# A pre-norm scan and mixture-of-experts kernel: a new order of rounding, remainders, routing steps and mixing, and two more PSUM banks for a quad's down part

## The chip, the cores and the metric

The kernel runs on one core of one Trainium2 chip. The metric is the device time of one execution in microseconds (us), the median over runs; lower is better. TensorE is the matrix engine, VectorE, ScalarE and GpSimd are the other compute engines, and SyncE (SP) issues most of the transfers.

## What is computed

The input is 4 x 1024 tokens of 256 features. Two blocks follow one another, each on a layer-normed copy of its input and added to it. The reference, cut to what matters:

```python
def attn(x, w_qkva, gamma):
    h = rmsnorm(x, gamma)                     # 256 features
    q, kv, a = split(h @ w_qkva.T)            # 256 each
    a = sigmoid(a)
    y = associative_scan(lambda l, r: (r.a * l.a, r.a * l.kv + r.kv), (a, kv), axis=1)
    return q * y
def ffn(x, router_w, w_gate, w_up, w_down, sw_gate, sw_up, sw_down):
    logits = x @ router_w.T                   # 7 experts
    top_vals, top_idx = top_k(logits, 2)
    w = softmax(top_vals)
    y_e = (silu(x @ w_gate[e]) * (x @ w_up[e])) @ w_down[e]    # hidden size 1024
    return sum of w * y_e over a token's two experts + the same with sw_* (shared expert)
x = x + attn(layernorm(x), ...)
x = x + ffn(layernorm(x), ...)
```

All of it is in float32.

## The kernel before

**Precision.** A matrix product in float32 is made of three products of rounded operands (float32r): hi x hi, hi x lo and lo x hi, where hi is the rounded value and lo the remainder. Rounding is ScalarE's work (`round_w`, `x_hi`, `h_hi`), remainders are VectorE's and GpSimd's. `w_both` holds an expert's rounded weights and their remainders for gate, up and down (parts 0, 1, 2); there are two such buffers. `w_raw` lies in the place of the remainders: the raw weights land there and are turned into the remainders in place. The loads of the next expert but one can start when a buffer's gate and up parts have been used.

**Stages.** Behind the scan block come in this order: two shared slots and four shared quads (the shared expert on 256 and 512 tokens at a time), two lone blocks (128 tokens of one expert each, plain float32), one more shared quad ("LATE"), four lone blocks, twelve routed quads, eight routed single slots, and two shared quads as the tail. A slot is 256 sorted tokens of one expert, a quad 512.

**A quad** has eight steps over the hidden size (128 each), then the down part. In step j TensorE makes gate and up with 12 matmuls of 512 columns (L1127) into banks 0 to 3, ScalarE the silu (L844), VectorE the product h32 (`gate`, L1700), ScalarE the rounded `h_hi` (L849), VectorE the remainder `h_lo` (`rest`, L1706). TensorE may be two steps ahead of the product. In the early quads h32 lies in SBUF, in the others in bank 7. In two of the steps VectorE transposes the next tokens' rows (`turn_x`, L1330) into bank 6, ScalarE rounds them (`x_hi`), VectorE makes their remainder (`x_lo`, L1344). The down part has two halves of two tiles. The first (`down_wide`) uses banks 4 and 5: one matmul of 512 columns takes h_hi against rounded weights and remainders side by side (L1105), one of 256 adds h_lo x hi (L1108). The second half works in bank 6 alone, with three matmuls of 256 columns (L1146).

**The order written out by hand.** Each engine's program is a list with waits on semaphores. ScalarE rounds the next expert's weights in a routed quad behind `h_hi` of steps 0 to 5: up, up, gate, gate, down, down. VectorE makes the remainder of up in two halves (`split_half`, L1661) behind steps 3 and 4, in a single slot behind the fourth pair. GpSimd does, per quad: `gather_ahead` of one unit (indirect DMA, L642), the remainder of gate (`split_lo`, L618), the second gather, the remainder of down, then two scatters of finished rows (L655). `scatter_y` also gives ScalarE leave to fill `y_rows` again (`y_free`). SP puts gathered rows to DRAM, loads them back in the layout for the transposition, and then issues the next weights: up, gate (L412), and down (L418).

**y of a routed quad.** ScalarE copies the remainder columns of banks 4 and 5 (L861), VectorE adds the others (L1773); of bank 6 ScalarE copies all (L865).

**Routing.** VectorE chooses the experts, ranks the tokens and moves their places (`rank_kinds` to `shift`), then makes lists of rows by one-hot matmuls: eight chunks of eight tiles (`hot_rows`, `hot_cols`), which TensorE multiplies in `list_part` (L1058), in bank 7. `take_lists` writes the row numbers of the gathers (L1625), `take_targets` those of the scatters, `owners` the experts of the slots. All are spread between the steps of the quads 2, 4 and 6.

**Tail.** In the two last quads SP fetches each token's two expert rows (`load_got`, L538 and L541), in four rounds of 6, 12, 12 and 2 tiles. ScalarE multiplies them by their weights (`weigh`, L904), VectorE adds the two and then adds the sum to `resid` (`mix`, L1646 and L1648), and SP stores.

```python
for j in range(JH):                                       # ScalarE, a quad
    act.activation(silu...); act.wait_ge(gated, q + 3)
    act.activation(h_hi...)
    if nxt is not None and j < 6:
        round_w((1, 1, 0, 0, 2, 2)[j], nxt[0], nxt[1], j % 2)
```

## Time and profile before

| | us |
|---|---|
| median of 3 runs | 1114.69 (1114.10 to 1115.27) |
| the profiled execution | 1114.16 |
| its span on the core | 1112.4 |
| TensorE busy | 1019.9 (92% of the span) |
| VectorE busy | 637.9 (57%) |
| ScalarE busy | 477.9 (43%) |
| GpSimd busy | 407.6 (37%) |

A busy share is an average over stages. The granted clock says at which share of 2.4 GHz TensorE ran; at its lower level, 1.2 GHz, the value of a moment is 0.5. "Idle before" is the time that an engine stood still before an instruction, with the instruction that released it. Instructions of one engine overlap by about 0.1 us in the records.

### The profile page before, as it was taken

Reading aid. Unit: us, or ns where it says so; the run is one execution under the profiler, and the core shown is the slowest. Engines: PE = TensorE matmul, PEld = TensorE weight load, DVE = VectorE, ACT = ScalarE, POOL = GpSimd, SP = SyncE. Lnnn points to the kernel's source line nnn. Section 1 sums busy time; section 2 is a strip of 40 time slices with the busy share of each in tenths; the row PEclk is TensorE's granted clock in tenths of the full one; section 3 lists DMA queues with packets and bytes.
Section 4 is the critical chain, followed back from the end, with each engine's and each line's share of the span. In section 5 each row is a group of like instructions: output and inputs, shape, how many; then the busy total and the mean of one; then the engine's idle time right before and its main releaser. Section 6 shows DMA issues by size and latency. Waiting matters only on the chain.

```text
span 1112.4 us, 16252 instructions
## 1 busy us (share of the span) xinstructions
PE 1019.9 (92%) x5757; PEld 882.9 (79%) x5757; DVE 637.9 (57%) x1037; ACT 477.9 (43%) x778; POOL 407.6 (37%) x258
## 2 busy tenths in 40 slices
PE   7999999998999999999999999999999688888897
PEld 6788978877989978777877887787779677777776
DVE  7997677876333353464346444644553655656566
ACT  4554342231233244354435443543454444455474
POOL 3234000002101443554455345634653666445300
PEclk9999999999999999999999999999999988888899
DMA  8324110002865744424443444344434555343544
GB/s 293 95 77 113 41 28 10 20 1 82 255 246 179 269 158 166 152 85 160 165 142 94 165 160 141 95 165 165 133 96 168 175 214 198 132 155 118 180 143 142
DMA packets 145907, 155.08 MB, mean 139 GB/s; under 512 B 75321, under 2 KB 134210, under 8 KB 138690
## 3 DMA queue, kind: packets, MB, share of 16 engines
q1 hardware_dynamic: 139120, 136.08, 37.5%
q0 software_dynamic: 6720, 18.36, 5.1%
q8 instruction: 28, 0.46, 0.2%
q14 instruction: 21, 0.17, 0.0%
q10 hardware_dynamic: 18, 0.01, 0.0%
HBM read 127.67 MB, written 26.74 MB: 139 GB/s over the span
## 4 chain that ended last, share of the span: by engine, by line
PE 49%; DVE 23%; ACT 15%; issue 10%; DVEq 0%; DMA 0%; POOL 0%; SPq 0%; ACTq 0%
PE ps L1127 16%; PE ps L1146 9%; DVE ps L1700 7%; DVE w_both L1661 6%; PE ps L1105 5%; PE ps L1083 5%; PE ps L1166 4%; ACT w_both L788 4%; ACT h_hi L849 3%; PE ps L990 3%; ACT silu L844 3%; PE ps L1108 3%; PE ps L1174 2%; ACT silu L816 2%; DVE y_sb L1312 2%
## 5 line engine op out<-in xcount | busy, mean ns | idle before, releaser
L1127 PE MATMUL ps<-xs_hi,w_both 128*128 128x512 f32 x1216 | 402.8, 405 | 41.4 <-DVE ps L1700 33.5
L1127 PEld LDWEIGHTS ps<-xs_hi,w_both 128*128 128x128 f32 x1216 | 236.2, 194 | 108.1 <-DVE ps L1700 49.6
L618 POOL TENSOR_TENSOR w_both<-w_raw,w_both 128x2048 fp32r<-128x2048 f32 x45 | 227.3, 5058 | 95.0 <-ACT w_both L788 86.3
L1127 PE MATMUL ps<-xs_lo,w_both 128*128 128x512 f32 x608 | 243.4, 400 | 0.0
L1700 DVE TENSOR_TENSOR ps<-ps,silu 128x512 f32<-128x512 f32 x160 | 111.3, 696 | 191.8 <-ACT silu L844 135.4
L642 POOL DMA_INDIRECT x_stage<-z_rows,idx_x x70 | 82.1, 1173 | 296.4 <-DVE idx_x L1625 143.8
L1706 DVE TENSOR_TENSOR h_lo<-ps,h_hi 128x512 fp32r<-128x512 f32 x160 | 110.7, 692 | 106.9 <-ACT h_hi L849 85.5
L1105 PE MATMUL ps<-w_both,h_hi 128*128 128x512 f32 x464 | 165.5, 399 | 1.8 <-DVE h_lo L1706 1.8
L1083 PE MATMUL ps<-xs_hi,w_both 128*128 128x256 f32 x640 | 130.1, 303 | 32.8 <-DVE w_both L1661 32.0
L849 ACT ACTIVATE h_hi<-ps 128x512 fp32r<-128x512 f32 x128 | 76.6, 598 | 146.4 <-DVE ps L1700 146.4
L1083 PEld LDWEIGHTS ps<-xs_hi,w_both 128*128 128x128 f32 x640 | 110.6, 210 | 35.5 <-issue 35.4
L1127 PEld LDWEIGHTS ps<-xs_lo,w_both 128*128 128x128 f32 x608 | 118.5, 195 | 22.8
L844 ACT ACTIVATE silu<-ps 128x512 f32<-128x512 f32 x152 | 90.1, 593 | 103.4 <-PE ps L1127 103.4
L655 POOL DMA_INDIRECT expert_rows<-y_rows,idx_y x70 | 69.8, 997 | 175.4 <-DVE y_rows L1773 69.8
L788 ACT ACTIVATE w_both<-w_raw 128x1024 fp32r<-128x1024 f32 x126 | 130.8, 1051 | 0.0
L1108 PE MATMUL ps<-w_both,h_lo 128*128 128x256 f32 x464 | 130.4, 281 | 0.0
L1146 PE MATMUL ps<-w_both,h_hi 128*128 128x256 f32 x608 | 111.6, 286 | 0.0
L1661 DVE TENSOR_TENSOR w_both<-w_raw,w_both 128x1024 fp32r<-128x1024 f32 x42 | 106.8, 2558 | 0.0
L1105 PEld LDWEIGHTS ps<-w_both,h_hi 128*128 128x128 f32 x464 | 87.3, 188 | 23.5 <-DVE h_lo L1706 3.0
L1146 PEld LDWEIGHTS ps<-w_both,h_hi 128*128 128x128 f32 x608 | 95.8, 194 | 0.8
L1083 PE MATMUL ps<-xs_lo,w_both 128*128 128x256 f32 x320 | 96.2, 301 | 0.0
L1108 PEld LDWEIGHTS ps<-w_both,h_lo 128*128 128x128 f32 x464 | 87.8, 189 | 0.8
(222 smaller groups left out, 1166.2 us busy)
## 6 DMA issues: line engine op xcount, KB each, us to landing
w_raw<-in_L_ffn_w_up_dram SPq DMA_DIRECT2D x20, 1024.0 KB, 4.9
w_raw<-in_L_ffn_w_gate_dram SPq DMA_DIRECT2D x20, 1024.0 KB, 7.1
w_raw<-in_L_ffn_w_down_dram SPq DMA_DIRECT2D x20, 1024.0 KB, 5.5
sorted_rows<-x_stage SPq DMA_DIRECT2D x32, 256.0 KB, 2.2
x_rows<-sorted_rows SPq DMA_DIRECT2D x128, 64.0 KB, 1.9
w_spare<-in_L_ffn_w_up_dram SPq DMA_DIRECT2D x6, 1024.0 KB, 5.2
w_spare<-in_L_ffn_w_gate_dram SPq DMA_DIRECT2D x6, 1024.0 KB, 8.7
w_spare<-in_L_ffn_w_down_dram SPq DMA_DIRECT2D x6, 1024.0 KB, 9.6
```

The costliest lines, as they stand in the source:

```text
L618: pool.tensor_tensor(w_lo[buf][:, k, :], w_raw[buf][:, k, :], w_hi[buf][:, k, :].bitcast(F32), ALU.subtract).then_inc(wlo_ready[k], 1)
L788: ins = act.activation(w_hi[buf][:, k, cols], w_raw[buf][:, k, cols], ACT.Copy)
L844: act.activation(silu[:, par, :, :], ps[:, 2 * par, :].rearrange("p (j n) -> p j n", j=2), ACT.Silu).then_inc(silu_ready, 1)
L849: act.activation(h_hi[:, j, :].rearrange("p (j n) -> p j n", j=2), h32_of(par, early), ACT.Copy).then_inc(hhi_ready, 1)
L1083: last = pe.matmul(o, w[:, part, at[kd]:at[kd] + P], unit(xx, h)[:, kd, :], start=i == 0, stop=i == len(terms) - 1)
L1105: pe.matmul(ps[:, 4 + t, :].rearrange("p (b d) -> p b d", d=D), h_hi[:, j, t * P:(t + 1) * P], both[:, :, 2, j * D:(j + 1) * D], start=j = ...
L1108: last = pe.matmul(ps[:, 4 + t, 0:D], h_lo[:, j, t * P:(t + 1) * P], hi[:, 2, j * D:(j + 1) * D], start=False, stop=j == JH - 1)
L1127: last = pe.matmul(ps[:, 2 * (j % 2) + part, :], w[:, part, kd * H + j * P:kd * H + (j + 1) * P], xx[:, h // 2, kd, :], start=i == 0, stop ...
L1146: last = pe.matmul(ps[:, 6, (t - ST) * D:(t - ST + 1) * D], a[:, j, t * P:(t + 1) * P], w[:, 2, j * D:(j + 1) * D], start=j == 0 and i == ...
L1661: ins = dve.tensor_tensor(w_lo[buf][:, 1, cols], w_raw[buf][:, 1, cols], w_hi[buf][:, 1, cols].bitcast(F32), ALU.subtract)
L1700: dve.tensor_tensor(h32_of(par, early), up, silu[:, par, :, :], ALU.mult).then_inc(gated, 1)
L1706: dve.tensor_tensor(out, h32_of(par, early), hi.bitcast(F32), ALU.subtract).then_inc(h_ready, 1)
```

## The change

The numbers that follow are all in the diff.

- Rounding: in quads ScalarE rounds gate behind silu of steps 0 and 1, up behind silu of steps 3 and 4, and down behind the last step; in slots gate, gate, up, up behind the four silus. SP loads gate before up.
- Remainders: VectorE makes both halves of up behind the last step of a quad. GpSimd makes the remainder of gate ahead of the first gather.
- Down part: in all quads but the early ones the second half has the form of the first, in banks 6 and 7. ScalarE copies, and VectorE adds, as for the first half. The fourth shared quad becomes an early one.
- Routing: the lists use float16 and one value for a token in place of two, in groups of 16 tiles; the steps move to other places, and the last three groups (`take_lists`, `take_targets`, `owners`) too. SP issues `load_lone(1)` behind two loads of x.
- Mixing: VectorE does own tiles and round 0 with two scalar_tensor_tensor a tile; in rounds 1 and 2 ScalarE weighs the other tiles and GpSimd adds them.

```diff
@@ SP
-                for k in (1, 0):
+                for k in (0, 1):
                     sp.dma_start(parts_of(w_raw[b])[k], sources[k]).then_inc(raw_in[b][k], 16)
...
-            for i in range(2):
-                load_lone(i)
+            load_lone(0)
             for u in range(2):
                 load_x(LATE + u, SA - 2 + u, z_dram, u)
+            load_lone(1)
...
+            sp.wait_ge(mixed, TOP * (ST + OTHERS[0]))
+            store_others(0)
+            load_got(2)
+            store_own(0)
+            sp.wait_ge(mixed, TOP * (ST + OTHERS[0] + ST))
+            load_got(3)
+            store_own(1)
...
@@ GpSimd
+                split_lo(0, r + 2, 1 - r % 2)
                 gather_ahead(i + 4)
-                split_lo(0, r + 2, 1 - r % 2)
                 gather_ahead(i + 5)
                 split_lo(2, r + 2, 1 - r % 2)
                 scatter_y(i)
                 scatter_y(i + 1)
...
+            for j in (1, 2):
+                for b in range(2):
+                    many = OTHERS[j] // 2
...
+                    pool.wait_ge(weighed, TOP * done)
+                    pool.tensor_tensor(sums, sums, got[:, j % 2, ps_, 1, :], ALU.add).then_inc(others_summed, many)
+                    pool.wait_ge(others_summed, done)
+                    pool.tensor_tensor(rows, rows, sums, ALU.add).then_inc(others_mixed, many)
@@ ScalarE, slot
+                    if nxt is not None:
+                        round_w((0, 0, 1, 1)[p], nxt[0], nxt[1], p % 2)
                     act.wait_ge(gated, q + 3)
...
-                    if nxt is not None:
-                        round_w((1, 1, 0, 0)[p], nxt[0], nxt[1], p % 2)
@@ ScalarE, quad
+                    if nxt is not None and j in (0, 1, 3, 4):
+                        round_w(j // 3, nxt[0], nxt[1], j % 3)
                     act.wait_ge(gated, q + 3)
...
-                    if nxt is not None and j < 6:
-                        round_w((1, 1, 0, 0, 2, 2)[j], nxt[0], nxt[1], j % 2)
...
+                if nxt is not None:
+                    for half in range(2):
+                        round_w(2, nxt[0], nxt[1], half)
...
                     act.wait_ge(y_free, r + 1)
-                    act.wait_ge(down_free, n + 2)
-                    act.activation(y_rows[:, 1, :, :], ps[:, 6, :].rearrange("p (t d) -> p t d", d=D), ACT.Copy
-                                   ).then_inc(down_free, 1)
+                    act.activation(y_rows[:, 1, :, :], ps[:, 6:8, D:2 * D], ACT.Copy).then_inc(y_half, 1)
...
-            quad(NB0, NB0 % 4, between={4: lambda: weigh(0, range(0, 2)), 5: lambda: weigh(0, range(2, 4)),
-                                        6: lambda: weigh(0, range(4, 6))})
-            for p in range(0, 12, 4):
-                weigh(1, range(p, p + 4))
+            quad(NB0, NB0 % 4, between={6: lambda: weigh(1, (ST,)), 7: lambda: weigh(1, (ST + 1,))})
+            weigh(1, range(ST + 2, ST + OTHERS[1]))
             quad(NB0 + 2, (NB0 + 2) % 4, turns=(), between={
-                j: lambda j=j: weigh(2, range(2 * j - 2, 2 * j)) for j in range(1, 7)})
-            weigh(3, range(2))
+                j: lambda j=j: weigh(2, (ST + j,)) for j in range(JH)})
+            weigh(2, range(ST + JH, ST + OTHERS[2]))
@@ TensorE, quad, second half of the down part
                 for t in range(ST, 2 * ST):
                     for j in range(JH):
+                        if not early:
+                            last = down_wide(j, both, hi, (t,))
+                            continue
...
-                at = {2: {}, 4: {1: [0], 6: [1], JH: [2]}, 6: {1: [3], 2: [4], 6: [5], JH: [6, 7]}, 8: {}}[n]
+                at = {2: {}, 4: {1: [0], JH: [1]}, 6: {0: [2], 1: [3], 6: [4], JH: [5]}, 8: {0: [6], 2: [7]}}[n]
@@ VectorE, mixing
+                dve.wait_ge(got_in[u], (64, 64, 128, 96)[j])
+                first_of = mixes[0]
+                for k in range(TOP):
+                    for i, p in enumerate(ps_):
+                        if k:
+                            dve.wait_ge(mixed, first_of + i + 1)
...
+                        dve.scalar_tensor_tensor(out=row, in0=got[:, u, p, k:k + 1, :],
+                                                 scalar=mix_w[:, k, t:t + 1], in1=row,
+                                                 op0=ALU.mult, op1=ALU.add).then_inc(mixed, 1)
@@ VectorE, quad
-                    if nxt is not None and j in (3, 4):
-                        split_half(*nxt, j - 3)
+                    if nxt is not None and j == JH - 1:
+                        split_up(*nxt)
...
-                    dve.wait_ge(y_half, routed)
-                    dve.tensor_tensor(y_rows[:, 0, :, :], ps[:, 4:6, 0:D], y_rows[:, 0, :, :], ALU.add
-                                      ).then_inc(down_free, 1)
+                    for half in range(2):
+                        dve.wait_ge(y_half, routed + half)
+                        dve.tensor_tensor(y_rows[:, half, :, :], ps[:, 4 + 2 * half:6 + 2 * half, 0:D],
+                                          y_rows[:, half, :, :], ALU.add).then_inc(down_free, 1)
+                    dve.wait_ge(down_free, n + 3)
@@ VectorE, where the routing steps and the mixing stand
             betweens = {
-                2: {0: lone_targets, 2: find_pairs, 3: find_over, 4: move_pairs, 5: move_alone,
-                    6: move_over, 7: move_on, "down": rows_of_first, "half": first_lists},
-                4: {0: lambda: hot_rows(1), 3: lambda: hot_cols(1), 6: lambda: hot_rows(2), 7: lambda: hot_cols(2),
-                    "down": lambda: lists(3), "half": lambda: lists(4)},
-                6: {1: lambda: hot_rows(5), 3: lambda: hot_cols(5), 6: lambda: hot_rows(6), 7: lambda: hot_cols(6),
-                    "down": lambda: lists(7), "half": last_lists}}
+                2: {0: pair_targets, 3: lone_places, 6: lone_targets, 7: find_pairs, "down": move_all,
+                    "half": first_lists},
+                4: {0: lambda: hot_rows(1), 3: lambda: hot_cols(1), 7: lambda: pick(1),
+                    "down": lambda: (halves_of(1), lists(2)), "half": lambda: lists(3)},
+                6: {0: lambda: hot_rows(4), 3: lambda: hot_cols(4), 6: lambda: hot_rows(5), 7: lambda: hot_cols(5),
+                    "down": lambda: (lists(6), owners()), "half": lambda: lists(7)}}
...
-            quad(n, n % 4, turns=ahead_of(n), kind="lone", shared=n, skip=0)
+            quad(n, n % 4, shared=n, early=True, skip=0, between={
+                3: take_lists, 6: take_targets, "down": lambda: turn(n, n % 4, 2, loads(n + 2), 0, "lone"),
+                "half": lambda: turn(n, n % 4, 3, loads(n + 3), 0, "lone")})
...
             quad(NB0, NB0 % 4, turns=ahead_of(NB0), shared=SA, between={
-                5: lambda: mix(0, range(0, 2)), 7: lambda: mix(0, range(2, 6)),
-                "half": lambda: mix(1, range(0, 2))})
+                6: lambda: mix(0, (0,)), 7: lambda: mix(0, (1,)), "down": lambda: mix(0, range(2, 6)),
+                "half": lambda: mix(1, (0, 1))})
...
+                4: lambda: mix(2, (0,)), 5: lambda: mix(2, (1,)), 6: lambda: mix(3, (0,)), 7: lambda: mix(3, (1,))})
```

## Rows read from the trace of the kernel before

**Rows 1.** Busy time by stage: early quads 2 to 6, fourth, routed, slots, tail.

```profile
core 0: us, PE busy (x) PEld busy (x) DVE busy (x) ACT busy (x) POOL busy (x), PEclk, DMA share, GB/s
148.50:262.98 114.48, 108.12 (x594) 90.46 (x593) 90.41 (x184) 32.25 (x55) 2.31 (x2) 0.99 0.05 12
262.98:296.17 33.19, 33.19 (x179) 28.70 (x178) 14.74 (x29) 9.58 (x16) 4.04 (x4) 1.00 0.79 239
392.79:844.85 452.06, 420.94 (x2115) 351.76 (x2114) 218.88 (x300) 200.47 (x312) 223.83 (x119) 0.97 0.43 142
844.85:1032.67 187.82, 151.24 (x1026) 143.18 (x1025) 112.14 (x112) 90.30 (x129) 106.73 (x41) 0.89 0.46 158
1032.67:1112.40 79.73, 70.42 (x352) 58.57 (x352) 48.40 (x67) 44.59 (x98) 6.14 (x3) 0.97 0.50 162
```

**Rows 2.** Who TensorE waited for: us in total, times, longest.

```profile
PE ps L1127 <- DVE ps L1700: 33.5, 16, 2.5
PE ps L1083 <- DVE w_both L1661: 32.0, 7, 4.6
```

**Rows 3.** The chain that ended last, in two routed quads: start, us, what.

```profile
603.91 4.44 PE ps L1127 x12
...
613.99 5.76 PE ps L1146 x48
619.75 2.76 PE ps L1127 x12
```

**Rows 4.** VectorE in a routed quad, timeline: start, us, instruction.

```profile
600.27 2.98 DVE L1661 TENSOR_TENSOR w_both<-w_raw,w_both 128x1024 fp32r<-128x1024 f32 x1
603.17 0.69 DVE L1700 TENSOR_TENSOR ps<-ps,silu 128x512 f32<-128x512 f32 x1
```

**Rows 5.** VectorE, GpSimd and SP in single slots, timeline.

```profile
883.17 6.69 DVE L1661 TENSOR_TENSOR w_both<-w_raw,w_both 128x1024 fp32r<-128x1024 f32 x2
...
883.56 10.71 POOL L618 TENSOR_TENSOR w_both<-w_raw,w_both 128x2048 fp32r<-128x2048 f32 x2 [2.71 <-ACT w_both L788]
...
903.28 1.03 POOL L642 DMA_INDIRECT x_stage<-z_rows,idx_x  x1 [0.30 <-issue]
...
910.86 0.37 SPq L412 DMA_DIRECT2D w_raw<-in_L_ffn_w_up_dram  x1
```

**Rows 6.** ScalarE in a routed quad, timeline.

```profile
624.59 1.06 ACT L788 ACTIVATE w_both<-w_raw 128x1024 fp32r<-128x1024 f32 x1
625.53 0.59 ACT L844 ACTIVATE silu<-ps 128x512 f32<-128x512 f32 x1
626.98 0.60 ACT L849 ACTIVATE h_hi<-ps 128x512 fp32r<-128x512 f32 x1 [0.85 <-DVE ps L1700]
```

**Rows 7.** GpSimd's second remainder in a routed quad, timeline.

```profile
605.52 4.62 POOL L618 TENSOR_TENSOR w_both<-w_raw,w_both 128x2048 fp32r<-128x2048 f32 x1
```

**Rows 8.** DMA issues of the page: count, KB each, median us from issue to landing.

```profile
w_raw<-in_L_ffn_w_up_dram SPq DMA_DIRECT2D x20, 1024.0 KB, 4.9
w_raw<-in_L_ffn_w_gate_dram SPq DMA_DIRECT2D x20, 1024.0 KB, 7.1
...
w_spare<-in_L_ffn_w_gate_dram SPq DMA_DIRECT2D x6, 1024.0 KB, 8.7
```

**Rows 9.** Timeline: the lists done; the first lone weights issued.

```profile
257.90 0.20 DVE L1625 CAST idx_x<-rows_f 128x70 int32<-128x70 f32 x1
...
274.16 0.36 SPq L447 DMA_DIRECT2D w_spare<-in_L_ffn_w_up_dram  x1
```

**Rows 10.** Two stretches of the tail, columns as in rows 1.

```profile
1054.00:1056.00 2.00, 2.00 (x11) 1.65 (x10) 1.81 (x3) 2.00 (x6) 0.00 (x0) 1.00 0.96 303
...
1076.00:1078.00 2.00, 2.00 (x10) 1.65 (x10) 1.33 (x3) 1.49 (x4) 0.00 (x0) 1.00 0.72 247
```

**Rows 11.** Timeline: a scalar_tensor_tensor of the routing; the fetch of round 2.

```profile
179.06 0.48 DVE L1534 SCALAR_TENSOR_TENSOR tmp<-keep,over_to,tmp 128x256 f32<-128x256 f32 x1
...
1064.66 0.36 SPq L538 DMA_DIRECT2D got<-expert_rows  x1
```

More of the change, by code:

```diff
@@ L1100, in slot, with down_wide @@
                 last.then_inc(down_psum, 1)
-            def down_wide(j, both, hi):
-                for t in range(ST):
+            def down_wide(j, both, hi, tiles=range(ST)):
+                for t in tiles:
                     pe.matmul(ps[:, 4 + t, :].rearrange("p (b d) -> p b d", d=D),
```

149 lines of the change are left out of this document (74 added, 75 removed).

## The prediction

> **What bounds the kernel now.** I read the stages first, then who makes TensorE wait, then one routed quad engine by engine. The table by stage [rows 1] shows TensorE busy nearly all the time in every stage, so the way to look is what its best pace is and which stages miss it. The shared quad from 262.98 has no gap at all: 33.19 us, clock 1.00. That is the floor of a quad of four tiles. The twelve routed quads take 452.06 us, 37.67 each, so 4.5 above the floor. The eight single slots take 187.82, or 23.48 each. The waits [rows 2] name the losers: 33.5 us in 16 waits for the gating product on VectorE (L1700), 32.0 in 7 of up to 4.6 for the remainder of the up weights (L1661).
>
> Inside a routed quad the chain [rows 3] gives the pace: twelve matmuls of 512 columns take 2.76 us, but 4.44 after the long wait (the engine was idle before it and runs at the lower level, 1.2 GHz, for a while), and the 48 matmuls of the second down half 5.76. So a quad loses 2.5 us of waiting and 1.7 of low clock. VectorE [rows 4] shows the cause: after step 4 it starts the second half of the up remainder at 600.27, and it takes 2.98 instead of 1.2, since GpSimd is in its own remainder; the next gating product starts only at 603.17. The same in the slots [rows 5]: two halves take 6.69 on VectorE while GpSimd does 10.71 for two remainders. One engine's operation stands still for the whole of the other's, in turn. TensorE, done with the slot before, waits 4.6 for them [rows 2].
>
> **The change part by part.** Times below count from TensorE's start of the quad or slot; pace 2.72 a step in a quad, 2.88 a pair in a slot (11.5 for the whole gate and up part, then 5.65 of down).
>
> *Routed quads.* ScalarE's silu and h_hi take 0.6 each, a rounding half 1.05, and between silu and h_hi it now waits 0.85 for the product [rows 6]. Put in that wait, a rounding half costs 0.2 more than nothing; silu, rounding and h_hi are 2.3 us of a 2.72 step, and the two steps with an x_hi have no rounding. VectorE has two operations of 0.7 a step, and in four of eight steps one more of about that length (transposition or x_lo): at most 2.2 of 2.72 without the remainder. The up remainder goes to the end: h_lo of step 7 ends at 24.8, both halves at 27.2, while TensorE is in the down part until 33.1. So the wait of 2.5 and the low clock of 1.7 are gone. What is late next: GpSimd's second remainder waits for the two rounding halves at the end (26.0), yields to VectorE until 27.1, and takes 4.6 [rows 7], to 31.7; only then does it reach the scatter that lets ScalarE copy the second half of y (needed at 33.2). That holds with 1.5 us. With y in banks 6 and 7 VectorE must also add the second half (34.0 to 34.7) before it may write bank 7 in the next quad, whose first gating product isn't due before 36.7: hidden. The 32 matmuls in place of 48 stream the same columns; the first half does that in 33.19-8x2.72-5.76=5.67, so 0.1 is gained. Gather and transfer: the fifth step's transposition ends at 17.5, gathers at 20.0, and 6.55 us later (gather end 904.31 to the issue at 910.86 [rows 5]) the gate weights are issued, at 26.6; the first of two loads lands in 4.9 [rows 8], at 31.5, and is wanted at 36.8. Hidden by 5 us. New quad: 33.1. 12 x (37.67-33.1) = **-54.9**.
>
> *Slots.* VectorE's remainder starts at 14.75, before GpSimd asks (16.05), and ends at 17.15, just when TensorE finishes (17.17). Without more a slot takes 17.2. But the gather now stands behind the gate remainder, and this closes a ring: gate weights land, two roundings with h_hi and silu between (3.15), remainder 4.6, two gathers 2.5, put, load and issue 6.55, landing 4.9: 21.8 us from one load to the next. ScalarE stands at the first rounding from 3.7 until the landing at 8.9, so everything behind it is late: rounding 1.05, h_hi 0.6, silu of the second pair 0.6 and its product 0.7, so TensorE's fourth pair starts at 12.0 instead of 8.6; with 2.9 for the pair, 1.4 of low clock after a wait of 3.4 and 5.65 of down part the slot ends at 21.9. Slots 1 to 4 hang on gathers and take 21.9; slot 0 has its weights from the quads, and slots 5 to 7 load rows that need no gather: 17.2. 4x17.2+4x21.9=156.4. **-31.4**.
>
> *Shared quads and routing.* The three quads with the lists take 114.48 [rows 1]. Each chunk loses one of VectorE's two products, and most steps move behind the gate part. I count 34.1 (the steps that stay, twelve or so of 0.2 and two of 0.45, leave 0.9 of lateness over 33.2), 37.9 (the first list chunk is made 2.3 us after TensorE wants it, plus 1.5 of low clock, plus two list parts of 0.5, estimated from eight times 140 columns at the pace of 2.76 for twelve times 512) and 35.1 (four list parts; the owners' steps, which held VectorE between the down halves, fit before the next quad's first product): 107.1, **-7.4**. The fourth quad pays 1.2 for two list parts and for taking the lists at step 3. There the lists come late: done at 17.3 of that quad. Before, SP issued the first lone expert's weights 16.3 us after the lists (257.90 to 274.16 [rows 9]): now at 33.4, when TensorE is nearly done (34.4). Landing takes 7.1 to 9.1 (gate is second: 7.1 with w_raw, 8.7 for w_spare [rows 8]), so TensorE waits 7.6 and pays 1.4 of clock. **+10.2**. The second lone expert's weights follow behind eight loads of x, by 304 of the trace's time, before they are wanted at 309.
>
> *Tail.* N is its start; today it takes 79.73. The fetches of y's rows keep the DMAs busy until 1056, N+23.4 [rows 10]. ScalarE now asks for round 1 in step 6 (N+21.3) and waits 2.4; five of its tiles are weighed at N+30. VectorE mixes by scalar_tensor_tensor, 0.5 each (0.48 in the routing [rows 11]): 12 for round 0, eight of them done by N+30. Then GpSimd starts its adds, 4.62x1280/2048=2.9 each. If these two block one another like the remainders [rows 5], each of VectorE's last four operations lets one add by: done at N+43; then 1.4+2+1.4 more, so the last quad's first product ends at N+48.7, where TensorE wants it at N+39.1. The fetch of round 2 starts at N+43.3, lands some 12.7 later as now (1064.66 to about 1077.4 [rows 10, 11]), at N+56, and ScalarE stands before it, so step 3 starts at N+58.3. Five steps, the down part, 1.4 of clock and 1.7 of one more block end TensorE at N+86.3, the last adds and the store take 5: N+91.3, **+11.5**. No row shows scalar_tensor_tensor against GpSimd: without a block the same count gives N+78, -1.7. I take the first, since the nearest row is the remainder, also two operands from SBUF.
> The Trainium skill ("SBUF — State Buffer", Who interferes with whom) says that any VectorE instruction with two SBUF inputs contends with a GpSimd instruction that reads SBUF, whole instruction for whole instruction. The trace agrees for tensor_tensor [rows 5]; by the rule the tail is +11.5, and GpSimd's help with mixing is a loss.
>
> Sum: -54.9-31.4-7.4+10.2+11.5 = -72.0. The profiled execution is 1114.16 (span 1112.4 and 1.8 around it), 0.5 under the median of the runs: 1114.2-72 = **1042**.
>
> **The rivals.**
> 1. Tail without the block (a scalar operand form might take turns more finely). For: no row shows it. Against: the remainders. 1042-13=1029.
> 2. The ring in the slots doesn't bind, because load or gather is shorter than its rows: 1042-4x4.7=1023. Against: every term has a row, and 4.9 is already the first load's median [rows 8].
> 3. The quads keep a part of their wait: product and remainder of h meet the transposition in steps 1 and 4 (VectorE is 0.4 to 0.6 late there, against 1.3 of slack). One wait of 1.3 a quad: +16, 1058; if it also draws the low clock (1.7), 1078.
> 4. The slower side: bank 7. Its chain in a quad is GpSimd reaching the scatter (31.7), y copy 0.6, y add 0.7, gating product 0.7, with some 0.3 between; TensorE wants that product at 38.5, so it costs from 36.2 on, one for one. To give back 72 us it has to be 6.0 a quad, so GpSimd at 42.2, 10.5 later than counted: 1114 and more. That is two further whole remainders; against it speaks that GpSimd is busy 223.83 us in twelve quads [rows 1], 18.7 of 33 each.
> 5. The change doesn't do it: the wait in the quad comes from something other than VectorE's order, as a late load. Against: the product starts the moment the remainder ends (603.17) [rows 4]. 1114-31-5=1080 or so.
>
> **How the numbers follow.** The sum as worked out 50% (1042); rival 1 15%, rival 2 8%, rival 3 20%, rivals 4 and 5 with other mishaps 7%. Bounds of the unknown terms: tail -13 to +3, lone load -2 to +3, first list chunk -4, landing in the ring up to 7.1 instead of 4.9 (+9). From 1018 to 1066 lie rivals 1 and 2, the first half of 3, and these bounds; the second half of 3 and rivals 4 and 5 are left out. A measurement here tells about 0.2%, 2 us, from no change; only rival 4, or several mishaps at once, reaches it: faster 0.96, same 0.01, slower 0.03.
>
> **What would show it.** Right: quads of 33.1 to 33.5 with clock 1.00 and no wait for L1700; up remainders of 1.2 each behind step 7; slots of 17.2, four of 22 whose ScalarE idles before a rounding; TensorE waiting once, 7 us, for the first lone weights; VectorE's mixing operations of 3 us beside GpSimd's adds in the tail. Wrong: a quad over 34.5, ScalarE idle before the second y copy (rival 4), or slots all at 17.

## The result, and the profile after

The changed kernel takes 1051.95 us (median of four runs, 1051.18 to 1052.50) against 1114.39 for the kernel before beside it: ratio 0.9441, 95% interval 0.9425 to 0.9457. The profiled execution took 1051.96, with a span of 1050.2. That is 62.2 us of span less; 72 were forecast. One of the four executions of experiment 9 below took 1967.32 us and is left out of its numbers; what held it up isn't known.

Busy time by stage of the changed kernel, columns as in [rows 1]: quads 2 to 6, the fourth shared quad, routed quads, slots, tail.

```profile
148.84:252.93 104.09, 102.33 (x586) 87.57 (x585) 79.78 (x161) 32.89 (x55) 0.00 (x0) 1.00 0.05 11
252.93:288.78 35.85, 34.28 (x190) 28.83 (x186) 21.96 (x46) 9.62 (x16) 5.34 (x5) 1.00 0.16 41
396.07:793.60 397.53, 397.53 (x1923) 334.00 (x1921) 206.96 (x311) 205.07 (x312) 216.47 (x119) 1.00 0.49 161
793.60:956.79 163.19, 146.27 (x1027) 139.08 (x1026) 78.12 (x112) 90.00 (x128) 101.91 (x41) 0.93 0.55 187
956.79:1050.20 93.41, 72.34 (x322) 58.78 (x320) 53.22 (x71) 36.27 (x75) 29.86 (x11) 0.90 0.42 138
```

Against [rows 1], in us of span, every stage from one profiled execution of each kernel:

| stage | before | after | measured | forecast |
|---|---|---|---|---|
| up to quad 2 | 148.50 | 148.84 | +0.3 | 0 |
| quads 2, 4, 6 (lists) | 114.48 | 104.09 | -10.4 | -7.4 |
| fourth shared quad | 33.19 | 35.85 | +2.7 | +1.2 |
| two lone blocks | 21.01 | 31.80 | +10.8 | +9.0 |
| LATE and four lone blocks | 75.61 | 75.49 | -0.1 | 0 |
| twelve routed quads | 452.06 | 397.53 | -54.5 | -54.9 |
| eight slots | 187.82 | 163.19 | -24.6 | -31.4 |
| tail | 79.73 | 93.41 | +13.7 | +11.5 |
| sum | 1112.4 | 1050.2 | -62.2 | -72.0 |

The routed quads are the easy reading: busy 397.53 of 397.53, clock 1.00, 33.13 each. Who TensorE waits for after the change (total, times, longest):

```profile
PE ps L1101 <- DVE ps L1733: 16.8, 4, 7.8
PE ps L1145 <- DVE ps L1733: 11.8, 3, 6.7
PE ps L1187 <- issue: 9.1, 1, 9.1
```

The 16 waits for the product in [rows 2] were 12 in the routed quads (30.2 us) and 4 in the tail (3.4). The 12 are gone, and so are the 7 for the up remainder and an eighth at the tail's start (4.6). In their place stand four waits in the slots (L1101), three in the tail (L1145) and one before the first lone block (L1187). The line named in the first two, VectorE's product, is only the last link; the causes follow.

**Slots.** The slots, counted from 0 as in the prediction, take 17.47, 27.96, 21.37, 23.55, 21.32, 17.20, 17.16 and 17.16. Slot 1 begins at 811.07. ScalarE there (timeline: start, us, instruction, idle before):

```profile
814.24 0.60 ACT L837 ACTIVATE silu<-ps 128x512 f32<-128x512 f32 x1 [2.61 <-PE ps L1101]
824.76 1.06 ACT L809 ACTIVATE w_both<-w_raw 128x1024 fp32r<-128x1024 f32 x1 [9.92 <-DMA w_raw<-in_L_ffn_w_gate_dram]
```

GpSimd and SP ahead of it:

```profile
801.67 0.97 POOL L664 DMA_INDIRECT expert_rows<-y_rows,idx_y  x1 [7.12 <-DMA expert_rows<-y_rows,idx_y]
802.95 0.98 POOL L664 DMA_INDIRECT expert_rows<-y_rows,idx_y  x1 [0.30 <-issue]
803.95 4.65 POOL L627 TENSOR_TENSOR w_both<-w_raw,w_both 128x2048 fp32r<-128x2048 f32 x1
808.76 1.88 POOL L651 DMA_INDIRECT x_stage<-z_rows,idx_x  x1 [0.16 <-issue]
810.94 1.03 POOL L651 DMA_INDIRECT x_stage<-z_rows,idx_x  x1 [0.30 <-issue]
...
814.61 0.40 SPq L457 DMA_DIRECT2D sorted_rows<-x_stage  x1
...
819.45 0.37 SPq L414 DMA_DIRECT2D w_raw<-in_L_ffn_w_gate_dram  x1
```

This is the ring of the prediction: remainder, gathers, rows to DRAM and back, and only then the next weights, which land at 824.7 while ScalarE and all behind it stand still.

**Tail.** VectorE and GpSimd, timeline:

```profile
984.43 12.28 DVE L1679 SCALAR_TENSOR_TENSOR resid<-got,mix_w,resid 128x256 f32<-128x256 f32 x10
...
998.27 2.66 DVE L1679 SCALAR_TENSOR_TENSOR resid<-got,mix_w,resid 128x256 f32<-128x256 f32 x4
...
987.13 3.10 POOL L714 TENSOR_TENSOR got<-got 128x1280 f32<-128x1280 f32 x1 [23.84 <-ACT got L924]
990.38 2.96 POOL L716 TENSOR_TENSOR resid<-resid,got 128x1280 f32<-128x1280 f32 x1
993.30 3.13 POOL L714 TENSOR_TENSOR got<-got 128x1280 f32<-128x1280 f32 x1
996.58 2.88 POOL L716 TENSOR_TENSOR resid<-resid,got 128x1280 f32<-128x1280 f32 x1
```

Ten mixing operations take 12.28. The first seven are over at 987.41, 2.98 after the start and just when GpSimd begins; the other three last 3.20, 3.17 and 3.17, each ending 0.3 after one of GpSimd's adds. With nothing on GpSimd beside them (experiment 8) the same ten take 4.16:

```profile
987.53 4.16 DVE L1667 SCALAR_TENSOR_TENSOR resid<-got,mix_w,resid 128x256 f32<-128x256 f32 x10
```

### The profile page after: what moved, and what is told of

Same layout as the page of the kernel before. It is cut to its first block, busy times and chain, and to the rows that moved or that the text cites. A ratio compares the mean times of both kernels' runs of the same rounds, so it can differ in the third digit from the quotient of the medians.

```text
span 1050.2 us, 15774 instructions
## 1 busy us (share of the span) xinstructions
PE 990.5 (94%) x5517; PEld 859.6 (82%) x5517; DVE 594.0 (57%) x1048; ACT 474.5 (45%) x754; POOL 419.2 (40%) x267
## 4 chain that ended last, share of the span: by engine, by line
PE 67%; DVE 11%; issue 8%; POOL 5%; DMA 4%; ACT 2%; SPq 1%; DVEq 0%; POOLq 0%; ACTq 0%
PE ps L1145 32%; PE ps L1123 11%; PE ps L1126 6%; PE ps L1101 5%; PE ps L1187 4%; PE ps L1007 3%; POOL w_both L627 3%; PE ps L1195 2%; DMA got<-expert_rows 2%; DVE y_sb L1333 2%; PE ps L991 1%; DVE resid L1679 1%; PE ps L1167 1%; DVE h_early L1733 1%; DVE h_lo L1739 1%
## 5 line engine op out<-in xcount | busy, mean ns | idle before, releaser
L1145 PE MATMUL ps<-xs_hi,w_both 128*128 128x512 f32 x1216 | 384.7, 394 | 12.5 <-DVE ps L1733 11.8
L1145 PEld LDWEIGHTS ps<-xs_hi,w_both 128*128 128x128 f32 x1216 | 230.6, 190 | 63.2 <-DVE ps L1733 13.1
L1123 PE MATMUL ps<-w_both,h_hi 128*128 128x512 f32 x704 | 250.2, 399 | 1.0 <-DVE h_lo L1739 0.9
L1145 PE MATMUL ps<-xs_lo,w_both 128*128 128x512 f32 x608 | 238.6, 392 | 0.0
L1126 PE MATMUL ps<-w_both,h_lo 128*128 128x256 f32 x704 | 197.5, 281 | 0.0
L651 POOL DMA_INDIRECT x_stage<-z_rows,idx_x x70 | 73.1, 1044 | 240.4 <-DVE idx_x L1651 156.4
L1123 PEld LDWEIGHTS ps<-w_both,h_hi 128*128 128x128 f32 x704 | 132.5, 188 | 33.6 <-DVE h_lo L1739 1.8
L1101 PE MATMUL ps<-xs_hi,w_both 128*128 128x256 f32 x640 | 126.3, 296 | 17.7 <-DVE ps L1733 16.8
L809 ACT ACTIVATE w_both<-w_raw 128x1024 fp32r<-128x1024 f32 x126 | 130.5, 1053 | 25.1 <-DMA w_raw<-in_L_ffn_w_gate_dram 25.0
L1145 PEld LDWEIGHTS ps<-xs_lo,w_both 128*128 128x128 f32 x608 | 115.5, 190 | 23.4
L1126 PEld LDWEIGHTS ps<-w_both,h_lo 128*128 128x128 f32 x704 | 133.0, 189 | 0.7
L1101 PEld LDWEIGHTS ps<-xs_hi,w_both 128*128 128x128 f32 x640 | 106.6, 202 | 19.8 <-DVE ps L1733 17.6
L1101 PE MATMUL ps<-xs_lo,w_both 128*128 128x256 f32 x320 | 93.9, 293 | 0.0
L1101 PEld LDWEIGHTS ps<-xs_lo,w_both 128*128 128x128 f32 x320 | 64.7, 202 | 0.0
L1809 DVE TENSOR_TENSOR y_rows<-ps,y_rows 128x512 f32<-128x512 f32 x24 | 16.6, 692 | 75.2 <-ACT y_rows L888 59.5
L1187 PE MATMUL ps<-xs_lone,w_spare 128*128 128x128 f32 x384 | 45.5, 281 | 9.1 <-issue 9.1
```

What stands on the lines that cost most here:

```text
L651: pool.indirect_dma_start(x_stage[:, i % 2, t, :], None, z_dram, bass.IndirectOffsetOnAxis(ap=idx_x[:, c:c + 1], axis=0), bounds_check=N - ...
L809: ins = act.activation(w_hi[buf][:, k, cols], w_raw[buf][:, k, cols], ACT.Copy)
L1101: last = pe.matmul(o, w[:, part, at[kd]:at[kd] + P], unit(xx, h)[:, kd, :], start=i == 0, stop=i == len(terms) - 1)
L1123: pe.matmul(ps[:, 4 + t, :].rearrange("p (b d) -> p b d", d=D), h_hi[:, j, t * P:(t + 1) * P], both[:, :, 2, j * D:(j + 1) * D], start=j = ...
L1126: last = pe.matmul(ps[:, 4 + t, 0:D], h_lo[:, j, t * P:(t + 1) * P], hi[:, 2, j * D:(j + 1) * D], start=False, stop=j == JH - 1)
L1145: last = pe.matmul(ps[:, 2 * (j % 2) + part, :], w[:, part, kd * H + j * P:kd * H + (j + 1) * P], xx[:, h // 2, kd, :], start=i == 0, stop ...
```

## The experiments

The changed kernel is the base of every run but where said; line numbers shift by a few between them. The kernel before had medians of 1115.15 beside experiments 1 to 4, 1114.31 beside 6, 7, 8 and 10, 1114.50 beside 9, 11 and 12, and 1113.51 beside 5.

**1. The quads with the old order.**

```diff
# ScalarE, quad
-  round gate behind silu of steps 0, 1; up behind silu of 3, 4; down at the end
+  round behind h_hi of steps 0 to 5: up, up, gate, gate, down, down
# VectorE, quad
-  if nxt is not None and j == JH - 1: split_up(*nxt)
+  if nxt is not None and j in (3, 4): split_half(*nxt, j - 3)
```

> The changed kernel, with ScalarE's rounding and VectorE's up remainder of the routed quads in the old places (rounding behind h_hi of steps 0 to 5 as up, up, gate, gate, down, down; up remainder behind steps 3 and 4). Theory: this order is where the 54 us of the quads came from. A quad goes from 33.1 back to 37 to 38 us, twelve of them 47 to 56 us: 1099 to 1108 us in all. Rival (banks 6 and 7 or GpSimd's order gave a part): under 1090 us.

Measured: 1118.15, ratio 1.0023 (1.0007 to 1.0039). The routed quads take 461.87, 38.49 each, even 0.8 more than before. With this part of the change undone all the gain is given back, and more than the 1099 to 1108 that were expected. VectorE and GpSimd in one quad of this run:

```profile
606.05 1.22 DVE L1691 TENSOR_TENSOR w_both<-w_raw,w_both 128x1024 fp32r<-128x1024 f32 x1
...
609.83 2.97 DVE L1691 TENSOR_TENSOR w_both<-w_raw,w_both 128x1024 fp32r<-128x1024 f32 x1
612.73 0.69 DVE L1730 TENSOR_TENSOR ps<-ps,silu 128x512 f32<-128x512 f32 x1
...
606.44 5.28 POOL L627 TENSOR_TENSOR w_both<-w_raw,w_both 128x2048 fp32r<-128x2048 f32 x1 [11.62 <-ACT w_both L809]
```

The block of [rows 4] is back within a hundredth: 2.97 for the second half, since GpSimd is in the remainder of gate until 611.72. But a block of 2.5 and 1.7 of low clock make 37.3, not 38.5. Something else is in here too; experiment 5 shows what.

**2. Only VectorE's remainder back between the steps.**

```diff
-  if nxt is not None and j == JH - 1: split_up(*nxt)
+  if nxt is not None and j in (4, 5): split_half(*nxt, j - 4)
```

> The changed kernel, with only VectorE's up remainder of the quads moved, behind steps 4 and 5. Two readings of the old wait: (a) VectorE had no room for 2.4 us between its steps, then a wait returns wherever it stands in the gate part; (b) only the block by GpSimd's remainder (2.98 us in place of 1.2) made it too long. In the new order GpSimd is in its gathers at steps 4 and 5, so by (b) each half takes 1.2 us, VectorE is 0.9 late at step 5 against 1.3 of slack, and the quad stays at 33.1 to 33.4 us: 1050 to 1056 us in all. By (a) a quad is 35 us or more: over 1074 us.

Measured: 1054.07, ratio 0.9453 (0.9435 to 0.9472); the quads 399.16, 33.26 each. With gate rounded first GpSimd's remainder of gate is over before VectorE starts:

```profile
581.02 1.20 DVE L1694 TENSOR_TENSOR w_both<-w_raw,w_both 128x1024 fp32r<-128x1024 f32 x1
...
584.70 1.22 DVE L1694 TENSOR_TENSOR w_both<-w_raw,w_both 128x1024 fp32r<-128x1024 f32 x1
...
573.03 4.64 POOL L627 TENSOR_TENSOR w_both<-w_raw,w_both 128x2048 fp32r<-128x2048 f32 x1
```

So it was never a matter of room on VectorE. With gate rounded first, the place behind the last step, to which the prediction gave the whole gain of a quad, is worth 0.13 a quad.

**3. The rounding behind h_hi again, in the new order.**

```diff
-  if nxt is not None and j in (0, 1, 3, 4): round_w(...)
   act.wait_ge(gated, q + 3)
   act.activation(h_hi...)
+  if nxt is not None and j in (0, 1, 3, 4): round_w(...)
```

> The changed kernel, with only ScalarE's rounding of the quads moved back behind h_hi (still gate in steps 0 and 1, up in 3 and 4, down at the end). Theory: silu, a wait of 0.85, h_hi and rounding are 3.1 us of a 2.72 us step; two such steps in a row make silu 0.4, then 0.8 late, still inside TensorE's slack of 1.3 a step, so the quad stays at 33.1 to 33.5: 1050 to 1056 us in all. Rival: the place inside ScalarE's wait carries much of the quads' gain, 35 us a quad or more: over 1074 us.

Measured: 1053.15, ratio 0.9445 (0.9426 to 0.9464), quads 397.53: the same to the hundredth. Filling ScalarE's idle time with the rounding, as the changed kernel does, is of no use here, since ScalarE isn't what ends last.

**4. The second down half in bank 6 alone, as before.**

```diff
-  if not early: last = down_wide(j, both, hi, (t,)); continue     # TensorE
-  copy of ps[:, 6:8, D:2*D], VectorE adds ps[:, 6:8, 0:D]
+  ScalarE copies ps[:, 6, :] whole
```

> The changed kernel, with the second half of every down part back in bank 6 (48 matmuls of 256 columns, ScalarE copies it whole, VectorE adds nothing). Theory: only the shorter stream counts, 0.1 us a quad, 14 quads: 1.4 us slower in all, 1052 to 1055, and the tail's last adds 0.7 shorter. Rival: the wide form costs by its second add or by bank 7 as a gate for the next quad: then this version is faster, under 1050 us.

Measured: 1052.83, ratio 0.9433 (0.9407 to 0.9459); the quads 398.44, 33.20 each: 0.07 more in each, so 0.9 for all twelve. That is the 0.1 of the prediction, and less than the runs can tell apart.

**5. The old rounding order, VectorE's remainder at the end.** The fourth corner of the first two runs.

```diff
# ScalarE as in experiment 1; VectorE as in the changed kernel
```

> The changed kernel with the quads' rounding as before (behind h_hi of steps 0 to 5: up, up, gate, gate, down, down), but VectorE's up remainder left behind the last step. With the run that moved only the remainder (quads 33.2) and the one that undid both (38.5), this is the fourth corner. Theory: the two edits are alternatives in the quads, since either keeps VectorE's remainder out of the time of GpSimd's remainder of gate while a gating product is due. With up rounded first GpSimd's gate remainder runs from about 14 to 19 of the quad and the one of down from about 23 to 27, so VectorE's two halves at 24.8 are blocked by 2 or 3 us, but under the down part, where nothing waits for them before the next quad's first product at about 36: quads 33.1 to 33.4, time 1050 to 1055, ratio 0.942 to 0.947. Rival: the rounding order costs the quads something by itself (the gather and the loads come later, or ScalarE's six steps with a rounding are too full): quads over 34 and a time over 1063.

Measured: 1103.40, ratio 0.9902 (0.9882 to 0.9923); the quads 448.17, 37.35 each. The expectation fell and its rival held. No product waits for a remainder here, and yet each quad loses 4.2. The block itself is still there: at the end of the quad VectorE's first half takes 4.4 to 4.7, beside GpSimd's remainder of down, but under the down part of TensorE, where nothing waits for it. VectorE, ScalarE, GpSimd and SP in the quad from 582.88:

```profile
613.61 5.54 DVE L1691 TENSOR_TENSOR w_both<-w_raw,w_both 128x1024 fp32r<-128x1024 f32 x2
...
591.45 1.06 ACT L809 ACTIVATE w_both<-w_raw 128x1024 fp32r<-128x1024 f32 x1 [3.53 <-DMA w_raw<-in_L_ffn_w_up_dram]
...
602.48 4.62 POOL L627 TENSOR_TENSOR w_both<-w_raw,w_both 128x2048 fp32r<-128x2048 f32 x1 [8.55 <-ACT w_both L809]
...
620.92 0.36 SPq L414 DMA_DIRECT2D w_raw<-in_L_ffn_w_gate_dram  x1
621.38 0.38 SPq L414 DMA_DIRECT2D w_raw<-in_L_ffn_w_up_dram  x1
...
629.52 1.06 ACT L809 ACTIVATE w_both<-w_raw 128x1024 fp32r<-128x1024 f32 x1 [2.58 <-DMA w_raw<-in_L_ffn_w_up_dram]
```

It is the ring of the slots, closed in the quads. ScalarE rounds up first, but SP now loads up second. Up lands at 591.4; up and gate are rounded by 602.4; then the remainder of gate to 607.1, the gathers behind it to 612.3, and rows out and in until 620; up is issued at 621.4 and lands 8.1 later, at 629.5. That is 38.1 from landing to landing in this quad (37.35 a quad on average), longer than the 33.1 of TensorE's work. ScalarE stands for it in each quad (38.5 us in 12 waits), the product is late, TensorE waits 1.8 to 3.4 (L1142) in eleven of the twelve quads and pays in clock. In experiment 1 this wait is there as well (18.2 us in 12), on top of the block, which fits the 0.8 over the kernel before.

Two things make the ring longer than with gate first. GpSimd can start its remainder of gate 10.9 after the landing, when four halves are rounded, where in the changed kernel the two halves of gate are done 3.8 after the first begins (598.39 to 602.17). And what is rounded first is loaded second and lands 8.1 after its issue, where the first of a pair takes 5.0. With SP's order put back too the ring would be some 35.0 by these numbers, an estimate that no run tried. The edit also moves the rounding of down from the end back between the steps; that wasn't tried by itself either.

The four corners, all with the gathers behind the remainder of gate, us per routed quad:

| | remainder at the end | remainder between the steps |
|---|---|---|
| gate rounded first | 33.13 | 33.26 (experiment 2) |
| up rounded first | 37.35 (experiment 5) | 38.49 (experiment 1) |

**6. The first gather ahead of the remainder of gate, as before.**

```diff
# GpSimd, quad
+  gather_ahead(i + 4)
   split_lo(0, r + 2, 1 - r % 2)
-  gather_ahead(i + 4)
# GpSimd, slot
-  split_lo(0, r + 2, 1 - r % 2)
   if i + 4 < NS + ROUTED: gather_ahead(i + 4)
+  split_lo(0, r + 2, 1 - r % 2)
```

> The changed kernel, with GpSimd's first gather ahead of its gate remainder again, in quads and slots. Theory: in quads nothing changes (33.1 us). In slots the ring opens, but the gate remainder now runs when VectorE wants its up remainder, and the two block one another: VectorE's two halves take 6 us or more, TensorE waits 4 to 5 us a slot, 21 to 24 us each where there are gathers, 17 to 22 in the other four. In all 1050 to 1075 us. Rival: the order of these two makes no difference, 1050 to 1054 us with slots as now.

Measured: 1063.88, ratio 0.9545 (0.9527 to 0.9562). The quads don't care (33.13), the slots take 174.42 in place of 163.19. VectorE and GpSimd in a slot of this run:

```profile
837.54 9.54 DVE L1694 TENSOR_TENSOR w_both<-w_raw,w_both 128x1024 fp32r<-128x1024 f32 x2
...
835.76 9.09 POOL L627 TENSOR_TENSOR w_both<-w_raw,w_both 128x2048 fp32r<-128x2048 f32 x2
```

With the gathers first GpSimd comes late to its remainders and is in them when VectorE wants its own: two halves take 9.54 in place of 2.35, worse than [rows 5]. TensorE waits 5.7 to 6.9 for the remainder in the four slots with gathers, and these take 24.5 to 26.8, more than the 21 to 24 expected.

**7. The ring in the slots opened.** SP issues gate and up ahead of the rows.

```diff
   v = n + 4 - R0
+  if r + 2 <= TURNS: load_gate_up(r + 2, u, n + 1, ...)
   if v < ROUTED: put_and_load(v, u, v // 2)
   else: load_x(n + 4, SA + v - ROUTED, z_dram, u)
-  if r + 2 <= TURNS: load_gate_up(r + 2, u, n + 1, ...)
```

> The changed kernel, with SP issuing the gate and up loads of a single slot ahead of that slot's put and load of gathered rows (they wait for TensorE's gate part alone). Theory of the ring: gate weights land, remainder, gather, put, load, next gate weights closes a ring of about 22 us, which slots 1 to 4 hang on. Cut there, all eight slots take 17.2 to 18.5 us: the slots' 163 us become 138 to 146, 1027 to 1035 us in all. Rival (the transfers themselves, or GpSimd with 16 us of work a slot, set the pace): the slots stay over 20 us, over 1042 us in all.

Measured: 1026.83, ratio 0.9219 (0.9203 to 0.9234), 25.1 us less than the changed kernel. The slots of this run, columns as in [rows 1]:

```profile
795.59:933.27 137.68, 137.61 (x1027) 131.37 (x1026) 78.50 (x112) 90.06 (x128) 101.90 (x41) 1.00 0.67 221
```

17.2 each, no wait, clock 1.00. The weights never needed the rows; they only stood behind them in SP's program.

**8. No adds on GpSimd in the tail.** This run leaves out the adds of the other tiles of rounds 1 and 2, four adds of 5 tiles, so 20 in all (not 22, as the expectation says); its output is missing them.

```diff
-  pool.tensor_tensor(sums, ...); pool.tensor_tensor(rows, ...)      # L714, L716
```

> The changed kernel without GpSimd's adds of rounds 1 and 2 in the tail (22 tiles do not get their experts' part; SP stores them once ScalarE has weighed them). Theory of the block: VectorE's scalar_tensor_tensor stands still for each add of 3 us. Without them ten of them take 5 us instead of 12.3, the last quad's first wait of 6.7 us goes, the fetch of round 2 starts 7 us earlier, and the tail shrinks by 8 to 14 us: 1038 to 1044 us in all. Rival: the fetches set the tail's pace, and it shrinks by less than 4 us, over 1048 us.

Measured: 1039.97, ratio 0.9327 (0.9304 to 0.9350). The tail takes 78.49, where the prediction's count without a block gave 78. Of the 14.9 gained TensorE's end brings 10.6 (74.4 after the tail's start in place of 85.0), and what follows it 4.3 (4.1 in place of 8.4). So the run takes away the block and GpSimd's late end together; it doesn't price them apart.

**9. The mixing as before, all else new.**

```diff
-  scalar_tensor_tensor on VectorE, adds of rounds 1 and 2 on GpSimd
+  ScalarE weighs, VectorE adds with two tensor_tensor (L1646, L1648 of before); SP's stores as before
```

> The changed kernel with the tail's mixing as it was before the change (ScalarE weighs, VectorE adds with tensor_tensor, nothing on GpSimd, SP's order of stores as before); all else stays. If the tail's +13.7 (79.7 to 93.4) comes from the new division of the mixing, the tail takes 78 to 80 from the start of its first quad and the time is 1037 to 1040, ratio 0.931 to 0.934, with no VectorE operation over 1.5 us there. Rival: a part of it comes from what stands ahead of the tail (the shape of the second down half, the last scatters, y of the last slots coming late): then the tail stays over 83 and the time over 1042.

Measured: 1038.36, ratio 0.9311 (0.9282 to 0.9340). Its tail, and VectorE in it:

```profile
959.61:1037.00 77.39, 67.95 (x322) 55.14 (x320) 50.10 (x69) 45.17 (x99) 6.04 (x3) 0.99 0.51 167
```

```profile
1002.36 1.22 DVE L1658 TENSOR_TENSOR got<-got 128x1024 f32<-128x1024 f32 x1
1003.68 1.23 DVE L1660 TENSOR_TENSOR resid<-resid,got 128x1024 f32<-128x1024 f32 x1
```

Two operations of 1.22 serve four tiles, 0.61 a tile; the new form costs VectorE 0.8 to 1.0 a tile even undisturbed (4.16 for five tiles in experiment 8, 1.00 for one at 978.69 in the changed kernel), and 2.5 in the 12.28 for five. So the new mixing costs 16.0 of tail (93.41 against 77.39), and 13.6 of the median time; the stages ahead of the tail were 2.8 longer in this run's profile.

**10 and 11. The first lone weights ahead of the rows; then both.**

```diff
   sp.wait_ge(listed, 1)
+  sp.wait_ge(routed, 1)
+  load_lone(0)
   put_x, load_sorted of units 0 and 1; put_x of 2 and 3
-  sp.wait_ge(routed, 1)
-  load_lone(0)
   load_x of LATE; load_lone(1)             # e12: load_lone(1) right behind load_sorted(1)
```

> The changed kernel, with SP issuing the first lone expert's weights as soon as the lists are done (270.8), ahead of the puts and loads of gathered rows. Theory: they land some 9 us later, long before TensorE wants them at 288.8, so its wait of 9.1 us and about 1 us of low clock go: 1040 to 1044 us in all. Rival: the x rows then come late and TensorE waits for them in place of the weights: over 1048 us.

> The changed kernel with the first lone expert's weights issued ahead of the gathered rows, and the second's right behind the rows of the two lone blocks, ahead of the loads of x for the quad LATE. Theory: with only the first moved, 9 us of wait became 2.2 + 4.8, the second being TensorE's wait for the second expert's weights, issued at 299; issued at about 291.5 they land at 300.5, before TensorE wants them at 303.3. LATE then starts at 315 to 318 in place of 320.6 and the time is 1046 to 1050. Rival: the loads of x for LATE, now 1.5 us later and behind 3 MB, hold VectorE in the first lone block (its transposition stands ahead of the product of the third step), TensorE waits there instead, and the time stays within 1 us of 1052.

Measured: 1052.50, ratio 0.9458 (0.9435 to 0.9481), and 1050.76, ratio 0.9425 (0.9402 to 0.9448). LATE starts at 321.13 and 321.47, against 320.58 in the changed kernel and 321.45 to 322.97 in the nine other runs that leave this part alone: neither gains anything that these runs can tell. TensorE in the first of the two runs, then TensorE and VectorE in the second:

```profile
295.77 3.84 PE L1187 MATMUL ps<-xs_lone,w_spare 128*128 128x128 f32 x32 [2.16 <-DVE h_lone L1821]
...
308.14 9.47 PE L1187 MATMUL ps<-xs_lone,w_spare 128*128 128x128 f32 x64 [4.83 <-issue]
```

```profile
305.36 3.78 PE L1196 MATMUL ps<-w_spare,h_lone 128*128 128x256 f32 x8 [4.48 <-issue]
...
304.21 0.79 DVE L1352 STREAM_TRANSPOSE ps<-x_rows 128x256 f32<-128x256 f32 x2 [8.62 <-DMA x_rows<-z_rows]
304.90 0.40 DVE L1822 TENSOR_TENSOR h_lone<-ps,silu 128x256 f32<-128x256 f32 x1
```

The 9 us at the first block become 0.5, 2.2 and 4.8 in the one, the last at the second's weights. In the other they become 2.4, 4.5 and 1.1; the 4.5 are LATE's rows, because their transposition stands ahead of a product that TensorE wants. Why the sum hardly changes isn't settled. In the first run the DMA engines are only 0.31 and 0.37 busy from 285 to 290 and from 290 to 295, and full from 305 on, so it isn't the amount of data alone; the order and the waits in SP's program weren't varied further.

**12. The three together:** SP's order of experiment 7, the mixing of 9, the lone weights of 11.

> The changed kernel with three edits at once: in the slots gate and up of the next expert but one are issued ahead of the rows; lone weights early as in the run beside it; the mixing as before. If the three are independent (25.2 measured for the first, 13.7 and 3.5 expected), the time is 1052 - 42 = 1010, range 1007 to 1014, ratio 0.904 to 0.910. Rival: the scatters and the fetches of y, which come 25 us earlier against the same loads, collide with something that the slots' waits hid: 1016 or more.

Measured: 1011.30, ratio 0.9068 (0.9043 to 0.9093): 40.7 us less than the changed kernel, and faster than both. Quads, slots and tail of this run:

```profile
397.51:795.03 397.52, 397.52 (x1922) 333.99 (x1921) 206.91 (x311) 205.26 (x312) 216.53 (x119) 1.00 0.48 161
795.03:932.67 137.64, 137.58 (x1026) 131.36 (x1025) 78.49 (x112) 90.22 (x128) 100.60 (x41) 1.00 0.66 222
932.67:1010.10 77.43, 67.87 (x322) 55.13 (x320) 50.12 (x69) 45.22 (x99) 6.05 (x3) 0.98 0.51 167
```

The gains of the three runs add up (25.1 + 13.6 + 1.2 = 39.9); the last of them is within the noise.

## Why the prediction was right, and where it was off

The sum missed by 10 us (-72.0 against -62.2). The signs and the places of all terms were right. The largest miss in size is the slots (6.8 too good), then the tail (2.2), the lone weights (1.8) and the lists (1.5 too bad), and in the quads a part of the cause was not seen.

**Routed quads: size right, cause half seen.** -54.9 forecast, -54.5 measured. The wait of 2.5 and the low clock of 1.7 are gone, as counted. The step was "the up remainder goes to the end ... so the wait of 2.5 and the low clock of 1.7 are gone". Experiment 5 bears out that this place takes the block out of TensorE's way, but experiment 2 shows that it isn't needed: gate first does the same, since it puts GpSimd's remainder of gate at 604.2 to 608.9, nine microseconds into the quad, where VectorE has no remainder, whether its own stands at the end or between the steps (33.13, 33.26). And the new place isn't enough. With the gather behind the remainder of gate, as the change has it, only gate first keeps the ring of the weights short; with up first it takes 37.35 a quad and bounds it. The prediction had the ring of the quads, hidden by 5 us, but didn't say that this hangs on the order of rounding. That the number came right without this is in part luck: the change held the edit that the sum gave no price. (Gate was issued at 27.8 of the quad in place of 26.6; with the median landing of 5.0 it is there 3.8 before ScalarE rounds it at 36.6.) One corner stays open: up rounded first, the gather ahead as before, and only VectorE's remainder moved wasn't tried, so whether that single edit on the kernel before would have done is not known.

**The details behind the quads** held. Behind the last step VectorE's two halves take 2.35 and GpSimd's remainder, beside them for a while, 5.48; it ends at 626.4, 31.5 into the quad, against 31.7 counted. Rival 3 (product late beside the transposition) did not come: L1145 waits in no quad. Rival 4 neither.

**Slots: -31.4 forecast, -24.6 measured.** The ring is right, and so is its length at rest: slots 2 and 4 take 21.37 and 21.32 against 21.9. The term that was mis-sized is its start. In the slot from 793.60 GpSimd can't begin the remainder of gate at 801.1, when gate is rounded, but at 803.95, since the scatter ahead of it waits 7.12 for the landing of the scatters before: +2.8. The gathers take 0.9 more than the 2.5 counted (one of them 1.88), the way from their end at 811.97 to the issue at 819.45 is 7.5 in place of 6.55, the landing 5.3 in place of 4.9. Together 5.0. Slot 1 is 6.1 over 21.9: its wait is 7.85 where 3.4 was counted, 4.4 more, and the other 1.6 I put to TensorE's clock after it (0.93 over the stage), which costs about 2.9 in this slot where 1.4 was counted. Slots 3 (23.55) and 0 (17.47) add 1.9, and slots 2 and 4 take off 1.1. In the runs that leave the slots alone slot 2 takes 21.3 to 23.6 and slot 3 21.3 to 23.9, so how these two come out is noise. Rival 2 (the ring doesn't bind) is refuted by experiment 7.

**Lists: -7.4 and +1.2 forecast, -10.4 and +2.7 measured**, -7.7 in all where -6.2 was counted: 33.22, 36.16 and 34.71 for the three quads against 34.1, 37.9 and 35.1. The bound named for the first list chunk was nearer: TensorE waited 1.76 in place of 2.3 and drew no low clock. In the fourth shared quad it waits 0.86 and 0.70 for products, which the sum didn't have.

**Lone weights: +9.0 forecast, +10.8 measured.** The lists are done at 270.79 and the weights issued at 287.04, 16.25 later, as before (16.3). TensorE waits 9.12 where 7.6 was counted. The second of the group's loads was issued at 287.50 and TensorE starts at 297.90, 10.4 later (the median landing of w_spare's gate is 9.5 after the change), where 7.1 to 9.1 was taken.

**Tail: +11.5 forecast, +13.7 measured.** The block was argued from the remainder alone, since no row of before had a scalar_tensor_tensor beside GpSimd. The rows show it directly (three operations of 3.2 in place of 0.4), and 78.49 without the adds and 77.39 with the old form agree. TensorE ends at 1041.8, 85.0 after the tail's start, where 86.3 was counted. Two misses cancel there: its wait in step 3 of the last quad ends at 55.3, not 58.3, and from there it takes 29.7, not 28.0. But then 8.4 are left, not 5. SP's last part:

```profile
1006.54 36.94 SPq L525 DMA_DIRECT2D out_dram<-resid  x2
1043.52 1.99 SPq L531 DMA_DIRECT2D out_dram<-resid  x2
```

The store of the other tiles of round 2 (1280 KB) can only go when GpSimd's last add ends at 1043.08, and the own tiles' stores queue behind it. So 1.8 MB leave at the very end, in 6.9 us. The prediction looked at the last matmul and the last adds on VectorE, not at what GpSimd finishes last. Rival 1 (no block) is refuted.

The Trainium skill ("SBUF — State Buffer", Who interferes with whom) says that a VectorE instruction with two inputs from SBUF contends with a GpSimd instruction that reads SBUF, and that the port pair they share is an exclusive lock. The 12.28 us agree, with a form that takes a scalar from SBUF as well. Which engine pays is also in the rows: here the three VectorE operations wait out an add that has begun, and GpSimd's adds are hardly longer for it (3.10, 2.96, 3.13 and 2.88, against 2.96 and 2.93 alone at 1037.05 and 1040.15). Where VectorE is first, behind the last step of a quad, it is the other way round: its two halves keep their 1.22 each, and GpSimd's remainder takes 5.48 in place of 4.62.

```profile
619.63 2.35 DVE L1694 TENSOR_TENSOR w_both<-w_raw,w_both 128x1024 fp32r<-128x1024 f32 x2
...
620.97 5.48 POOL L627 TENSOR_TENSOR w_both<-w_raw,w_both 128x2048 fp32r<-128x2048 f32 x1 [5.63 <-ACT w_both L809]
```

## What to carry to other kernels

Two engines that lock one another should be kept apart by time, and there are two ways: move the blocked operation to where nothing waits for it, or change what releases the other engine, here which part is rounded first. Both worked against the block; only the second also kept the loads early. Before an operation is put ahead of another in a queue, follow it once around: if what stands behind it gates, over other engines and DRAM, its own next input, it closes a ring whose length must be compared with TensorE's work; the cure is to issue what doesn't need the ring (here the weights) ahead of it. And work given to a second engine has to be counted to the last store that waits for it.

## What the runs showed of the hardware that was not expected

- The block isn't always in turn. In experiment 6 GpSimd's two remainders follow one another without a gap (from 835.76 and from 840.34, until 844.85), and VectorE's first half, begun at 837.54, lasts through both: 8.4, the second then 1.21. The same happens in the two slots behind it (8.4 each). GpSimd loses nothing (4.65 and 4.51). In the tail VectorE gets its turn between two of GpSimd's adds, even where these follow one another without a gap (at 993.3, VectorE's operation ends at 993.62). The prediction counted one operation for one throughout; what decides between the two no run here tells.
- A pair of 1 MB loads issued 0.46 us apart lands one after the other: 5.0 for the first, 7.3 for the second (medians after the change), and [rows 8] have 4.9 and 7.1 with the two in the other order. In these rows it's the place in the pair that counts, not the tensor. Experiment 5 needs first what is loaded second, and that lands 8.1 after its issue.
- A scatter that waits for the landing of the one before held GpSimd for 5.4 to 7.3 us in eleven of the twelve quads (6.13 at 601.95), and 7.12 in slot 0 (801.67), which no bound engine noticed until a ring ran through it.
